# A four-stage expert kernel on one core: attention steps and the norms behind expert stage 2 placed one to three chunks further apart

## What is computed

```python
x = x + _L0_attn_ref(_layernorm(x), ...)   # scan over 256 tokens
x = x + _L0_ffn_ref(_layernorm(x), ...)    # 64 experts, top 8, and a shared one
x = x + _L1_attn_ref(_layernorm(x), ...)   # softmax over random features
x = x + _L1_ffn_ref(_layernorm(x), ...)    # 8 experts, top 2, squared relu
x = x + _L2_attn_ref(_layernorm(x), ...)   # linear attention and convolution
x = x + _L2_ffn_ref(_layernorm(x), ...)    # 4 experts, relu
x = x + _L3_attn_ref(_layernorm(x), ...)   # wkv recurrence
x = x + _L3_ffn_ref(_layernorm(x), ...)    # 8 experts, silu, "zone" routing
```

## Time and profile before

| | us |
|---|---|
| median of three runs (1954.51 to 1964.04) | 1958.83 |
| the profiled execution | 1963.8 |
| its span, first to last instruction | 1961.8 |

### The profile page before, as it was taken

How to read it: one execution, slowest core, us unless ns; L and a number is a source line. 1 busy time by engine, 2 the same in 40 slices (tenths; PEclk the granted TensorE clock), 3 DMA queues, 4 the chain that set the end, 5 groups by cost and what they waited for, 6 DMA issues and landing times.

```text
span 1961.8 us, 25458 instructions
## 1 busy us (share of the span) xinstructions
PE 1723.9 (88%) x8004; PEld 1314.2 (67%) x8004; DVE 1198.0 (61%) x2815; ACT 974.3 (50%) x1864; POOL 847.5 (43%) x852
## 2 busy tenths in 40 slices
PE   6989998659999998989999988888899888888799
PEld 6979997537767676767777655666665555555565
DVE  5552215658677767777776835544446666677765
ACT  3612002346556665665656567676545444445442
POOL 3842101225545454554555454443447666651100
PEclk9989558769999999999999989898999888889999
DMA  5001000168433333233324462231000101112233
GB/s 84 1 2 24 1 1 1 38 146 201 111 92 102 87 98 92 90 99 86 96 90 118 114 161 73 58 88 47 17 23 23 33 23 26 23 28 75 81 106 94
DMA packets 131182, 134.92 MB, mean 69 GB/s; under 512 B 56614, under 2 KB 75306, under 8 KB 131050
## 3 DMA queue, kind: packets, MB, share of 16 engines
q1 hardware_dynamic: 120904, 132.35, 25.3%
q10 hardware_dynamic: 10146, 0.94, 0.6%
HBM read 127.93 MB, written 5.31 MB: 68 GB/s over the span
## 4 chain that ended last, share of the span: by engine, by line
PE 36%; DVE 17%; ACT 11%; issue 7%; POOL 4%; DMA 2%; SPq 1%; DVEq 0%; ACTq 0%; POOLq 0%
PE ypsum L1122 7%; PE flow_G L100 4%; PE flow_G L102 3%; PE flow_G L101 3%; DVE flow_a L1666 2%; DVE flow_a L1672 2%; DVE flow_phi L1450 2%; DMA flow_raw<-in_L_ffn_expert_down_k 2%; POOL flow_alo L1753 2%; PE flow_U L100 2%; PE flow_U L101 2%; PE flow_U L102 1%; ACT flow_ahi L1152 1%; ACT xn_tokens L1184 1%; PE flow_side L100 1%
## 5 line engine op out<-in xcount | busy, mean ns | idle before, releaser
L1753 POOL TENSOR_TENSOR flow_alo<-flow_a,flow_ahi 128x512 fp32r<-128x512 f32 x264 | 342.0, 1295 | 345.6 <-ACT flow_ahi L1152 345.1
L100 PE MATMUL flow_G<-xn_hi,flow_hi 128*128 128x512 f32 x520 | 285.6, 549 | 49.5 <-DVE flow_a L1666 23.2
L1666 DVE TENSOR_TENSOR flow_a<-flow_G,flow_mask 128x512 f32<-128x512 f32 x256 | 175.7, 686 | 161.2 <-ACT flow_G L1326 137.9
L1326 ACT ACTIVATE flow_G<-flow_G 128x512 f32<-128x512 f32 x256 | 149.0, 582 | 140.2 <-PE flow_G L102 139.7
L101 PE MATMUL flow_G<-xn_lo,flow_hi 128*128 128x512 f32 x520 | 213.0, 410 | 0.0
L102 PE MATMUL flow_G<-xn_hi,flow_lo 128*128 128x512 f32 x520 | 211.7, 407 | 0.0
L1672 DVE TENSOR_TENSOR flow_a<-flow_U,flow_a 128x512 f32<-128x512 f32 x296 | 204.7, 691 | 9.9
L1152 ACT ACTIVATE flow_ahi<-flow_a 128x512 fp32r<-128x512 f32 x264 | 165.4, 627 | 85.3 <-DVE flow_a L1672 84.1
L1762 POOL TENSOR_TENSOR flow_b<-flow_b,flow_mask 128x512 f32<-128x512 f32 x96 | 127.1, 1329 | 147.3 <-ACT flow_b L1330 76.7
L100 PEld LDWEIGHTS flow_G<-xn_hi,flow_hi 128*128 128x128 f32 x520 | 102.7, 197 | 117.6 <-issue 44.6
L1762 POOL TENSOR_TENSOR flow_a<-flow_a,flow_mask 128x512 f32<-128x512 f32 x96 | 127.8, 1343 | 106.3 <-ACT flow_a L1330 54.7
(11 more groups left out here) (536 smaller groups left out, 3930.1 us busy)
## 6 DMA issues: line engine op xcount, KB each, us to landing
flow_mask<-mask_rows_top SPq DMA_DIRECT2D x512, 128.0 KB, 3.1
flow_mask<-mask_rows_top SPq DMA_DIRECT2D x64, 256.0 KB, 3.3
flow_mask<-mask_rows_zone SPq DMA_DIRECT2D x64, 256.0 KB, 3.2
flow_mask<-mask_rows_steps SPq DMA_DIRECT2D x32, 256.0 KB, 4.0
x<-in_L_attn_x SPq DMA_DIRECT2D x8, 256.0 KB, 5.5
flow_raw<-in_L_ffn_expert_gate_k SPq DMA_DIRECT2D x16, 128.0 KB, 3.6
flow_raw<-in_L_ffn_expert_up_k SPq DMA_DIRECT2D x16, 128.0 KB, 3.6
flow_raw<-in_L_ffn_expert_down_k SPq DMA_DIRECT2D x16, 128.0 KB, 4.1
```

The costliest lines, as they stand in the source:

```text
L100: pe.matmul(out, w_hi, x_hi, start=start, stop=False)
L1326: act.activation(gate, gate, ACT.Silu).then_inc(ev["r_done"], 1)
L1666: dve.tensor_tensor(out, G[at % 2].psum[:, :], weight, ALU.mult).then_inc(ev["t_done"], 1)
L1753: pool.tensor_tensor(alo[i][:, :], acts[i][:, :], ahi[i][:, :].bitcast(F32), ALU.subtract)\
```

## The change

Only numbers in the tables of offsets change; every instruction stays. The tables of attention 1 stay, but `place` draws its last steps (`affinities`, `choose`, `weights`, `rows` of groups 6 and 7) closer, with a factor of 0.6 in place of 0.85. For attention 3 of the last group all offsets beyond 14 shrink by a factor of 0.84. `MOE_STEPS` becomes one table for each stage: `y` 0.1 earlier everywhere, which moves it ahead of the activation of the chunk before; behind stage 2 `normalize` one and `x_turn`, `hi`, `lo` two chunks later; in stage 3 everything behind `y` 1.5 later.

```diff
+        if (kind, l, g) == ("att", 3, GROUPS - 1):
+            off = 14 + (off - 14) * 0.84
...
-            return post + off - 44 if off <= 52 else post + 12 + (off - 54) * 0.85
+            return post + off - 44 if off <= 52 else post + 12 + (off - 54) * 0.6
...
-def post_steps(at):
+def post_steps(at, more=0):
 
-    return {"pe": ((at + 1, "y_turn"), (at + 6, "x_turn")), "act": ((at + 5, "normalize"), (at + 7, "hi")),
-            "dve": ((at + 2, "add"), (at + 3, "moments"), (at + 8, "lo")), "pool": ((at + 4, "rstd"),), "sp": ()}
+    return {"pe": ((at + 1, "y_turn"), (at + 6 + more, "x_turn")), "act": ((at + 5 + more / 2, "normalize"), (at + 7 + more, "hi")),
+            "dve": ((at + 2, "add"), (at + 3, "moments"), (at + 8 + more, "lo")), "pool": ((at + 4, "rstd"),), "sp": ()}
...
-MOE_STEPS = joined(post_steps(3), {"act": ((3, "y"),), "sp": ((5.5, "store"),)})
+MOE_STEPS = [joined(post_steps(4.5 if l == 3 else 3, 2 * (l == 2)), {"act": ((2.9, "y"),), "sp": ((7, "store"),)}) for l in range(4)]
...
-        "pe": ((12, "project"), (13, "receptance"), (35, "affinities"), (42, "weights")),
+        "pe": ((14, "project"), (15, "receptance"), (40, "affinities"), (48, "weights")),
```

More of the change, by code:

```diff
@@ L655, in steps @@
             for g in range(GROUPS):
-                out += [(self.place("moe", l, g, off), name, "moe", l, g) for off, name in MOE_STEPS[engine]
+                out += [(self.place("moe", l, g, off), name, "moe", l, g) for off, name in MOE_STEPS[l][engine]
                         if l < 3 or name in LAST_STEPS]
@@ L699 @@
         "sp": ((61, "rows"),)}),
-    2: joined(post_steps(25.5), {
-        "pe": ((12, "project"), (16, "turn"), (18, "state"), (22, "attend"), (24, "convolve"), (25, "output"),
-               (38, "affinities"), (45, "weights")),
-        "act": ((13, "exponentials"), (17, "copies"), (25.5, "y"), (39, "affinities"), (46, "weights")),
-        "dve": ((14, "features"), (15, "sums"), (19, "state"), (23, "divide"), (40, "choose_0"), (41, "choose")),
-        "sp": ((47, "rows"),)}),
-    3: joined(post_steps(24.5), {
-        "pe": ((12, "project"), (13, "receptance"), (35, "affinities"), (42, "weights")),
-        "act": ((13, "values"), (16, "exponentials"), (17, "receptance"), (36, "affinities"), (38, "distances"),
-                (43, "weights")),
-        "dve": ((13, "peaks"), (14, "arguments"), (14.5, "receptance"), (18, "den"), (19, "num"), (21, "quotient_0"),
-                (22, "quotient_1"), (37, "choose_0"), (39.5, "choose")),
-        "pool": ((15, "exponent"), (17, "products"), (20, "numerator")),
-        "sp": ((44, "rows"),)}),
+    2: joined(post_steps(25.7), {
+        "pe": ((12, "project"), (16, "turn"), (18, "state"), (22.5, "attend"), (23.5, "convolve"), (25.2, "output"),
+               (39.5, "affinities"), (46.3, "weights")),
+        "act": ((13, "exponentials"), (17, "copies"), (25.7, "y"), (40.4, "affinities"), (47.3, "weights")),
+        "dve": ((14, "features"), (16, "sums"), (19, "state"), (23.5, "divide"), (41.4, "choose_0"), (42, "choose")),
+        "sp": ((48.3, "rows"),)}),
+    3: joined(post_steps(26.5, 2), {
+        "pe": ((14, "project"), (15, "receptance"), (40, "affinities"), (48, "weights")),
+        "act": ((15, "values"), (18, "exponentials"), (19, "receptance"), (41, "affinities"), (43, "distances"),
+                (49, "weights")),
+        "dve": ((15, "peaks"), (16, "arguments"), (16.5, "receptance"), (20, "den"), (21, "num"), (23, "quotient_0"),
+                (24, "quotient_1"), (42, "choose_0"), (44.5, "choose")),
+        "pool": ((17, "exponent"), (19, "products"), (22, "numerator")),
+        "sp": ((50, "rows"),)}),
 }
```

## The result

The changed kernel takes 1976.84 us (median of five runs, 1970.24 to 1979.00), the kernel before 1958.83 (five runs, 1954.51 to 1964.04). The ratio is 1.0084, with a 95% interval of 1.0059 to 1.0108: slower by 0.6 to 1.1%, where I had forecast 1.4% faster. All source lines of the changed kernel are two higher than before (L1414 is L1416 now, L884 is L886, L894 is L896, L1002 is L1004).

What follows compares the result with a forecast made beforehand. It took stage 2's period as a loop through DVE's in-order list, costed as DVE's busy time plus waits. Gains 13.5 + 4 + 4 + 4 + 1 = 26.5 us off the profiled 1963.8 gave 1937.3, so 1932 us for the runs, range 1900 to 1955.

Steps and rivals of the forecast that it cites:

- rival 1: Whole kernel: DVE keeps everything, stage 2's period returns to 47.9 us, other parts give half; 1952 us, chance 0.16.
- Stage 2, groups 3 to 7: Period falls from 47.9 to 45.2 us a group, a gain of 13.5 us over five groups (3 to 23).
- The two waits for ACT become 6.4: Stage 2 group: DVE's waits for ACT's `hi` and `exponentials`, 3.2 and 2.2 us before, become 6.4 together.
- 2.0 in small ones: Stage 2 group: DVE's remaining small waits, 2.0 us before and taken as 2.0 after.
- The rule on the shared port: Stage 2 group: POOL's 31.7 us and DVE's roughly 9 us of two-input work can't overlap, a floor of about 41 us.
- Group 2, 4 us: Stage 2's group 2, without `choose` yet: moving `x_turn` takes most of PE's 4.3 us idle, gaining 4 us (0 to 6).
- Attention 2, 4 us: Chunks 320, 328, 336, 344: `attend` ahead of `affinities` gains 1.0 us each, 4 us in all (-4 to 8).
- Stage 3, 4 us gained, -5 to 8: Stage 3: idle time at `y_turn` (2.5 us) and `x_turn` (3.5 us) goes, waits at `flow_U` may grow by 2.
- `y` 0.1 earlier, 1 us: Earlier `y` lets the next group's `down` start at once, 1.6 us in all of stage 0; taken as 1 us gained.
- My slower rival: Stretching of `choose` beside POOL runs away: 54 us a group in stage 2, 17 us slower, 1976 us; chance 0.12.

Runs made afterwards that it cites:

- e9: Changed kernel with the norms behind stages 2 and 3 back where they stood before, `choose` left at 44.5: 1973.30 us, ratio 1.0061 to the kernel before.
- e3: Changed kernel with attention 3's `choose` 0.6 chunk later (45.1), behind `add` and `lo`: 1934.96 us, ratio 0.9864 to the kernel before.
- e12: e7 with `num` behind `moments`, so `numerator` behind `rstd`, and both quotients one chunk later: 1908.82 us, ratio 0.9725 to the kernel before.
- e4: Changed kernel with attention 3's `choose` at 49, in DVE's wait for the exponentials, `weights` and `rows` 3.5 later: 1939.66 us, ratio 0.9887 to the kernel before.
- e1: Kernel before with only attention 2's table, attention 1's last steps and the earlier `y` as in the change: 1961.78 us, ratio 0.9998.
- e14: e7 with attention 2's table, attention 1's last steps and `y` as in the kernel before: 1932.00 us, ratio 0.9849 to the kernel before.
- e5: Changed kernel with `choose` at 45.1 in attention 3's group 5 alone (chunk 470): 1970.25 us, ratio 1.0059 to the kernel before.
- e7: e3 with attention 3's `weights` and `rows` one chunk later: 1929.18 us, ratio 0.9836 to the kernel before.
- e2: Kernel before with only attention 3's table and the norms behind stages 2 and 3 as in the change: 1981.27 us, ratio 1.0113.
- e13: e12 with the norm behind stage 3 from 4 in place of 4.5: 1908.39 us, ratio 0.9734 to the kernel before.

## Why the prediction was wrong

Forecast 1932 us in 1900 to 1955, measured 1976.8. For stage 2 the period came out at that of rival 1, DVE keeps everything (0.16), but not by the stretching at its upper bound that it named: DVE's busy time was the forecast's. In stage 3 came a case that stood nowhere.

**Stage 2, groups 3 to 7.** The mechanism was right: the loop is `project`, DVE's list, `lo`, `project` (and the `add` of attention 3 holds `project` as `lo` does, which I hadn't seen; e9). The gaps are where I put them: none ahead of `weights` and `y_turn`, one of 5.6 us (forecast 4 to 7) ahead of `project`; only `x_turn`, with 2.4, is over its 2 us. The size was off. I had 33.7 busy and 11.5 idle on DVE, and measured 33.7 busy and 14.0 idle. The term that failed is "The two waits for ACT become 6.4" and its neighbours: the waits for ACT were 7.9, and that ahead of L1613 was 1.6, where 1.0 stood before among the "2.0 in small ones". The likely reason is that PE runs `project` at the lower clock behind its wait (0.63 us a matmul in place of 0.40): in e3, where `project` doesn't wait, the wait for the exponentials is 5.0 us in place of 6.1 and the one ahead of L1613 is gone. So a wait in the loop seems to lengthen the loop's own next steps; no run takes the clock apart from the order. The error is 2.5 us in 47.7, but the gain I was after was only 2.7: I had taken a small difference of two large sums. A group's period by that same sum said more than I drew from it: 7.5 of the 47.7 us were `choose`, for no reason but its place ahead of `add` and `lo`. I had named that and not asked what 0.6 chunk would do.

**The rule on the shared port.** The Trainium skill ("SBUF — State Buffer", section "Who interferes with whom") gave, with my estimate of DVE's two-input work, a floor of about 41 us for a group, "wherever the steps stand". e12's group 5 took 39.40 us. I had added POOL's whole busy time, 31.7, as if none of it were stretching. Of the 16 mask products of that group (L1764) four took 1.65 to 1.72 us, where the shortest takes 1.26; with the shortest duration of each of its instructions POOL comes to about 29 us there, and the floor to about 38 (an estimate). The 41 was wrong as a number. The rule itself the runs don't contradict: e4's rows on L1484 to L1486, with POOL at its products, lie 1.0 us above e3's.

**Group 2, 4 us.** Wrong sign: 43.3 against 42.4 (41.8 in e3 and 41.9 in e12, so at best 0.6 gained). Groups 0 and 1, which I had at nothing, gave 5.1 in the trace (111.9 to 106.8 us).

**Attention 2, 4 us.** The waits now stand ahead of `attend` alone, as forecast, 3.3 to 4.1 us at chunks 303, 311, 319 and 327 and 2.3 at 335 and 343 (it had 3.5 and 2.6 at the first two of them before, and none at the others). Stage 1 took 234.0 us in place of 237.1 in the trace. Over all traces it took 230.5 to 238.2 us in the eleven kernels with this part, 233.8 in the mean, and 235.9, 237.1 and 239.2 in the three without it, 237.4 in the mean. So the 4 us may be about right, but one execution differs from the next by more, and in the runs it can't be seen (e1, e14).

**Stage 3, 4 us gained, -5 to 8.** This step failed most: it lost 23.5. I had looked for what the moves take out of PE's waits, and found `y_turn` and `x_turn` correctly (2.5 and 3.5 us, both gone); the waits at `flow_U` kept within my 2 us, 17.4 in place of 16.6. I had not asked of the moved steps what they hold: `y_turn` of stage 3 claims the bank `turn` from `lo`, and that `lo` stands behind `choose` there too. I had drawn this loop for stage 2 and not carried it 15 chunks on. It is 8.6 us of wait; e5 takes 5.3 of them back. `weights`, next to `arguments` in the same bank, waits 3.9 us, 3.5 of them at chunk 457 (e7 takes that back), and `affinities` at chunk 481 waits 2.9 for an `add`. With 2.3 in small ones these are the 12.5 us of idle time: 8.6 + 3.9 + 2.9 + 2.3 + 0.8 - 2.5 - 3.5. The lower clock around the waits is 6.8 more. I had costed no clock in stage 3. And `choose` of group 6, now at chunk 488, makes one wait of 4.1 us there with 6.8 us of lower clock; no run moves that one alone.

**`y` 0.1 earlier, 1 us.** Nothing: chunks 33 to 263 took 633.5 us in e3, with it, and 633.1 in e2, without it.

**The chances.** My slower rival was drawn from stretching in `choose`, and gave 1976. The time agrees by chance: `choose` took 7.5 us, as before. "Slower" at 0.12 was too little, because none of my cases let stage 3 lose more than 5 us, though the steps of attention 3, of its norm and of the experts' norm had all been moved there.

## What to carry to other kernels

When steps of an in-order engine are moved apart, list for each wait on the critical path *everything* that its releaser now stands behind, banks as well as data, in each stage in which the pair meets; the next loop is as long as that list. A step whose result is needed late (`choose`) belongs behind those that release something early (`add`, `lo`), and 0.6 of a chunk of offset decided 42 us here. The distance that the change makes was right; it needed `choose` behind `lo`, `weights` clear of `arguments`, and `rstd` ahead of `numerator`, and then it is 2.7% faster than the kernel before (e12), not 0.8% slower.

## What the hardware showed that I had not expected

The clock took a larger share than I had given it: 6.8 of stage 3's 23.5 us. In the changed kernel PE has 3.4 or 6.8 us at the lower level (1.2 GHz) around the end of 25 of its 27 waits of 2.2 us or more between 420 and 1945 us. In groups 3 to 7 of e12 no wait is longer than 1.55 us, and it has none: the granted clock is 1.00, with PE busy 35.9 of 39.4 us. But it isn't fixed by the order: behind the wait of 3.7 us at chunk 470 e12 has no such stretch, and e13 one of 6.8 us.

And one profiled execution can be off in a place that has nothing to do with the change: 76.6 us for chunks 0 to 32 before and 76.4 in e9, 71.9 to 74.1 in the twelve other traces; and chunk 0 starts at 417.9 to 425.4 us, with the same program ahead of it.
